# Token blocks of two factors moved by separate transfers, and a projection done in two halves, in a fused two-layer attention kernel

## What is computed

```python
xn  = layernorm(x)
qu  = (xn @ U.T * s).reshape(b, t, C, R)        # U, V: (C*R, 128)
qv  = (xn @ V.T * s).reshape(b, t, C, R)
m   = einsum('bcsr,bctr->bcst', qu, qv)          # scores, 512 x 512 for each channel
h   = sigmoid(m)
o_v = einsum('bcst,bctr->bcsr', h, qv)
o_u = einsum('bcst,bcsr->bctr', h, qu)
x   = x + (o_v @ U + o_u @ V) * s + ffn0(xn)     # ffn0: routed experts, top 64 of 512 tokens each
x   = x + hss_attention(layernorm(x)) + swiglu(layernorm(x))
```

## Time and profile before

| what | value |
|---|---|
| median of three runs | 1467.37 us |
| the profiled execution, device time | 1468.4 us |
| its span, first to last instruction | 1466.6 us |
| mean granted TensorE clock | 0.98 |
| TensorE (PE) busy | 1389.9 us, 95% |
| VectorE (DVE) busy | 903.6 us, 62% |
| ScalarE (ACT) busy | 688.9 us, 47% |
| packets of the DMA queue that SP feeds | 302128, 19.4% of 16 engines' span |

### The profile page before, as it was taken

The page is one execution under the profiler, slowest core; times in us unless marked ns, Lnnn a source line. Parts: engine busy times, 40 slices in busy tenths (PEclk is TensorE's granted clock), DMA queues, the critical chain, the costliest instruction groups (busy, mean ns, idle before and its releaser), DMA issues.

```text
span 1466.6 us, 24503 instructions
## 1 busy us (share of the span) xinstructions
PE 1389.9 (95%) x7806; PEld 793.9 (54%) x7806; DVE 903.6 (62%) x1559; ACT 688.9 (47%) x1058; POOL 44.1 (3%) x41
## 2 busy tenths in 40 slices
PE   6999798899998999999999999999999999999968
PEld 3566444455564555555565555555655555555534
DVE  8868443366655665656655656556555666566657
ACT  3556344444443544454444543454544454454421
POOL 4000400000000000000000000000000000000000
PEclk9999899999999999999999999999999999999988
DMA  6012222112221212221112211221212111221110
GB/s 207 1 31 66 43 35 31 26 29 35 30 30 31 33 27 30 36 32 31 26 26 39 36 29 24 36 34 28 30 29 36 32 26 27 38 30 27 25 30 8
DMA packets 302620, 51.37 MB, mean 35 GB/s; under 512 B 280545, under 2 KB 300769, under 8 KB 302465
## 3 DMA queue, kind: packets, MB, share of 16 engines
q1 hardware_dynamic: 302128, 47.82, 19.4%
q0 software_dynamic: 336, 1.64, 0.3%
HBM read 11.64 MB, written 4.19 MB: 11 GB/s over the span
## 4 chain that ended last, share of the span: by engine, by line
issue 85%; DVE 1%; PE 1%; POOL 1%; ACT 0%; POOLq 0%; DVEq 0%
PE psum L1231 1%; DVE arena L917 0%; DVE arena L923 0%; DVE arena L915 0%; POOL u_w_hl L608 0%; POOL v_w_hl L608 0%; POOL rstd_s L623 0%; POOL up_hl L608 0%; DVE arena L939 0%; PE psum L1575 0%; DVE xn_s L663 0%; POOL u_w_hl L605 0%; POOL v_w_hl L605 0%; DVE x_all L932 0%; POOL up_hl L605 0%
## 5 line engine op out<-in xcount | busy, mean ns | idle before, releaser
L1172 ACT ACTIVATE arena<-psum 128x1024 f32<-128x1024 f32 x504 | 476.0, 1030 | 636.5 <-PE psum L1231 636.3
L1231 PE MATMUL psum<-arena 128*64 128x512 f32 x2016 | 466.0, 605 | 26.0 <-DMA arena<-blocks 14.6
L1231 PEld LDWEIGHTS psum<-arena 128*64 128x64 f32 x2016 | 135.0, 138 | 290.0 <-issue 244.7
L1231 PE MATMUL psum<-u_parts,v_parts 64*128 64x512 f32 x1536 | 199.5, 404 | 11.9 <-issue 11.2
L1231 PE MATMUL psum<-v_parts,u_parts 64*128 64x512 f32 (+1 forms) x1568 | 201.9, 397 | 0.0
L866 DVE TENSOR_SCALAR o_hl<-psum,sums 128x512 fp32r<-128x512 f32 x126 | 94.4, 749 | 162.1 <-PE psum L1231 162.1
L1231 PEld LDWEIGHTS psum<-u_parts,v_parts 64*128 64x128 f32 x1536 | 141.7, 187 | 93.1 <-issue 45.3
L1231 PEld LDWEIGHTS psum<-v_parts,u_parts 64*128 64x128 f32 (+1 forms) x1568 | 145.3, 184 | 81.5 <-issue 51.1
L868 DVE SCALAR_TENSOR_TENSOR o_hl<-psum,sums,o_hl 128x512 fp32r<-128x512 f32 x126 | 94.6, 751 | 4.5
L1121 ACT ACTIVATE arena<-psum 128x512 f32<-128x512 f32 x128 | 77.1, 625 | 18.5 <-PE psum L1231 18.5
L923 DVE TENSOR_TENSOR arena<-psum,arena 128x512 f32<-128x512 f32 x96 | 64.6, 689 | 33.7 <-PE psum L1231 31.7
(11 more groups left out here) (211 smaller groups left out, 1517.0 us busy)
## 6 DMA issues: line engine op xcount, KB each, us to landing
arena<-blocks SPq DMA_DIRECT2D x1008, 32.0 KB, 2.0
x_all<-in_x SPq DMA_DIRECT2D x4, 512.0 KB, 5.4
upper<-in_we SPq DMA_DIRECT2D x8, 256.0 KB, 2.7
expert_rows<-upper SPq DMA_DIRECT2D x16, 128.0 KB, 2.5
xn_s<-expert_rows SPq DMA_DIRECT2D x8, 256.0 KB, 2.9
out<-x_all SPq DMA_DIRECT2D x8, 256.0 KB, 2.5
arena<-in_e POOLq DMA_DIRECT2D x1, 896.0 KB, 5.7
arena<-in_wi POOLq DMA_DIRECT2D x1, 576.0 KB, 5.7
```

Of the source, the lines that this page charges most:

```text
L1172: nc.scalar.activation(th_of(un), psum[:, at:at + 2], ACT.Tanh, scale=0.5 * FACTOR_SCALE ** 2).then_inc(s_th, 2)
L1231: return nc.tensor.matmul(out, lhsT, rhs, start=start, stop=stop)
```

## The change

1. **Tokens.** `raw`, `tok` and `blocks` are split into u and v. Each even half turns v (128x512) and then u (128x512), and SP waits for each and moves it by 16 DMAs of its own, 16 KB each, from 32 to 32 partitions with 4 runs of 32 numbers on each. So a pair has 32 DMAs in place of 16, with the same bytes. `weighted` of the even half waits for v alone, that of the odd half for u. The turn of each waits for the landing of its own move before.
2. **First pair.** The tokens of pair 1 of batch 0 are no more turned and moved: TensorE transposes them (8 transposes into banks 2 and 3, put into the last expert) and ScalarE copies them to `u_tok` and `v_tok`.
3. **Projection.** `pj` becomes `pj0` (v part, o = 0, 3 matmuls) in the odd half of the same pair, and `pj1` (u part, o = 1, 3 matmuls) in the even half of the next, each in its own bank and added to `gT` by an instruction of its own.
4. **Loops on TensorE.** Batch 1 is written out, and batches 2 to 7 are three rounds of a loop with two batches.
5. **Layer 2.** gate and up of chunk 0 move from half 5 to half 3.
6. **Start.** The normalised rows of batches 1, 3, 5 and 7 are made by ScalarE (four ACTIVATE with scale and bias each, and a small VectorE instruction for the bias) and no more by VectorE; the router's products of two batches go to two groups of 32 rows of a bank.

```diff
-FULL_STEPS = {1: [("back", 0)], 2: [("norm", 0)], 3: [("kq", 0), ("v", 0)], 12: [("down", 0)], 15: [("yo", 0), ("yo", 1)]}
+FULL_STEPS = {1: [("back", 0)], 2: [("norm", 0)], 3: [("kq", 0), ("v", 0), ("gate", 0), ("up", 0)], 12: [("down", 0)], 15: [("yo", 0), ("yo", 1)]}
-PREP_IN_HALF = [("pu", "pv", "pj"), ()]
+PREP_IN_HALF = [("pu", "pv", "pj1"), ("pj0",)]
...
-            def move_tokens(i, j, blocks):
-                sp.wait_ge(s_turned, i * PAIRS + j + 1)
-                (16 DMAs, above)
+            def move_blocks(blocks, tok, moved):
+                for r in range(QUARTERS):
+                    for a in range(QUARTERS):
+                        sp.dma_start(tok[32 * r:32 * r + 32, :, 32 * a:32 * a + 32],
+                                     blocks[32 * a:32 * a + 32].rearrange("t (k r c) -> t k r c", k=TB, r=QUARTERS)[:, :, r])\
+                          .then_inc(moved, 16)
+            def move_tokens(i, j):
+                sp.wait_ge(s_vb, i * PAIRS + j)
+                move_blocks(v_blocks, v_tok[:, (j + 1) % 2], s_vt[j])
+                sp.wait_ge(s_ub, i * PAIRS + j)
+                move_blocks(u_blocks, u_tok[:, (j + 1) % 2], s_ut[j])
...
-                nc.vector.transpose(blocks.rearrange("p w t -> p (w t)"), raw.rearrange("p w t -> p (w t)")).then_inc(s_turned, 1)
+                nc.vector.transpose(blocks[:], raw[:]).then_inc(turned, 1)
...
-                        turn(i, j, later_blocks)
+                        turn(i, j, v_raw, v_blocks, s_vb, s_vt)
+                        turn(i, j, u_raw, u_blocks, s_ub, s_ut)
...
-            def project(g, j, bk):
-                pe.wait_ge(s_oe, g * 2)
-                was = (j - 1) % PAIRS
-                passes = [(o, a, b) for o in range(2) for a, b in ((0, 0), (0, 1), (1, 0))]
-                for n, (o, a, b) in enumerate(passes):
-                    ins = mm(bk[:], w_hl[o][:, a, was * D:(was + 1) * D], o_hl[:, o, b], n == 0, n == len(passes) - 1)
+            def project(kind, g, j, bk):
+                o, of = (0, j) if kind == "pj0" else (1, (j - 1) % PAIRS)
+                pe.wait_ge(s_oe, g * 2 + 1 if kind == "pj0" else g * 2)
+                for n, (a, b) in enumerate(((0, 0), (0, 1), (1, 0))):
+                    ins = mm(bk[:], w_hl[o][:, a, of * D:(of + 1) * D], o_hl[:, o, b], n == 0, n == 2)
...
-                if u == 0:
-                    pe.wait_ge(s_moved[(j - 1) % PAIRS], (i + (j > 0)) * MOVED)
+                if blk == 0 and isinstance(i, int) and i == 0 and j == 1:
+                    pe.wait_ge(s_prep_free, prep_index(0, 4) + 1)
+                elif blk == 0:
+                    pe.wait_ge((s_vt, s_ut)[o][(j - 1) % PAIRS], moved_count(i if j else i - 1, (j - 1) % PAIRS))
...
+            prep(0, 3, 1, 0, bank[2])
             attend(*last)
+            prep(0, 4, 1, 0, bank[3])
...
-            with pe.Fori(1, B) as i:
-                iteration(i, True, True)
+            iteration(1, True, True)
+            with pe.Fori(1, B // 2) as m:
+                for n in range(2):
+                    iteration(m * 2 + n, True, True)
```

More of the change, by code:

```diff
@@ L160, in first_middle_of @@
 def first_middle_of(h):
-    work = [w for w in MIDDLE[h] if w[0] in ("pu", "pv", "pj") and w != ("pj", 1)]
+    work = [w for w in MIDDLE[h] if w[0] in ("pu", "pv", "pj0", "pj1") and w != ("pj1", 1)]
     return work + [("sc", 0)] * (h == FIRST_SCATTER_HALF)
@@ L231, in scatter_bank @@
         def scatter_bank(i):
-            return x_bank(("sc", 0), not isinstance(i, int))
+            return x_bank(("sc", 0), not (isinstance(i, int) and i == 0))
         x_all = sb("x_all", [P, B, TB, D])
@@ L527, in _ @@
                 move_rows(E - 4 + par, E // 2 - 2, par)
-            def move_tokens(i, j, blocks):
-                sp.wait_ge(s_turned, i * PAIRS + j + 1)
[L531 to L539, removed]
+            for par in range(2):
+                move_rows(E - 2 + par, E // 2 - 1, par)
             def load_rows(n):
@@ L681, in part_rows @@
                 dve.wait_ge(s_rstd, h + 1)
[L682 to L685, removed]
+                odd, even = h * X_PART + 1, h * X_PART
+                nc.vector.scalar_tensor_tensor(shift1[:, odd], mv1[:, odd, :, 0], -1.0, rstd1[:, odd], ALU.mult, ALU.mult)\
+                  .then_inc(s_shift, 1)
+                if h:
+                    dve.wait_ge(s_xT, even - 1)
+                normalised(xn_g[:, 0], even, mv1[:, even, :, 0:1], rstd1[:, even].unsqueeze(2)).then_inc(s_xn, 1)
             nc.vector.memset(idle[:], 0.0).then_inc(s_ld, N_DVE)
@@ L727, in _ @@
             nc.vector.tensor_tensor(tk_rank, tk_pos, tk_mask, ALU.mult).then_inc(s_tk, 1)
[L729 removed]
+            rank_of, value_of = (rvT[:, a].rearrange("p k (g e b) -> p k g e b", g=2, e=E) for a in range(2))
             def low_rows(n, par):
@@ L855, in add_g @@
                     before = gT[:]
-                if isinstance(i, int) and i == 0 and j == 3:
+                if isinstance(i, int) and i == 0 and (kind, j) == ("pj1", 3):
                     dve.wait_ge(s_scf, 1)
+                if not (isinstance(i, int) and i == 0) and (kind, j) == ("pj0", 0):
+                    dve.wait_ge(s_scf, i + 1)
                 nc.vector.scalar_tensor_tensor(gT[:], bk[:], 0.5 * FACTOR_SCALE ** 2, before, ALU.mult, ALU.add).then_inc(s_pj_free, 1)
@@ L1233, in _, with transposes @@
             pe.wait_ge(s_first, 16 * len(first_consts))
-            def transposes(n, par):
-                pe.wait_ge(s_xn, n + 1)
-                if later(n):
+            def transposes(n):
+                par = n % 2
+                if par == 0:
+                    pe.wait_ge(s_xn, n // 2 + 1)
+                else:
+                    pe.wait_ge(s_xna, n // 2 + 1)
+                if n >= 2:
                     pe.wait_ge(s_xnT, n - 1)
@@ L1241, in transposes, with logits @@
                 ins.then_inc(s_xT, 1)
[L1243 to L1251 removed]
+            def logits(pair):
+                pe.wait_ge(s_xnT, 2 * pair + 2)
+                for g in range(2):
+                    ins = mm(bank[2][g * 64:g * 64 + 32], wr_b[:, pair * 32:pair * 32 + 32], xn1T[:, 2 * pair + g],
+                             pair == 0, pair == B // 2 - 1)
+                return ins
+            transposes(0)
+            transposes(1)
+            pe.wait_ge(s_wr, 2)
+            for n in range(2, B, 2):
+                transposes(n)
+                transposes(n + 1)
+                logits(n // 2 - 1)
+            logits(B // 2 - 1).then_inc(s_lg, 1)
             def early_prep(w, bk):
```

146 lines of the change are left out of this document (85 added, 61 removed).

## The result

The changed kernel takes **1567.5 us** (median of 4 runs, 1565.7 to 1571.6), the kernel before 1466.2 us beside it. The ratio is 1.0695 with a 95% interval of 1.0669 to 1.0721: 101 us, or 7%, slower. The forecast was 1570 us in a range of 1450 to 1612. Of all executions behind this document one, of the run e1_together, lay apart: 2024.7 us, where its seven others took 1469.3 to 1473.2; its ratio leaves that one out.

A forecast was written before the change was run, and what follows sets the result against it. TensorE bounds the kernel before; SP's serial DMA issue would bind after. Along SP: first move 166.3, 62 pairs of 21.6 (1339.2), other DMAs 5.2, landing 1.4, `weighted` 3.65, tail 53.05: 1568.8 us of span, forecast 1570, range 1450 to 1612.

The forecast's parts named there:

- SP becomes the bound, 21.6 us in a pair: SP's token queue: 32 issues of 0.598 us make a pair 21.6 us, where TensorE needs under 19.8; chance 0.72.
- What `expert_rows` and the tokens share is 64 or 32 partitions: SP's issue cost: it goes with partition count, not runs, so it stays near 0.611 us, against 0.387 to 0.432 over 128.
- The 50 ns of the Trainium skill: SP's dispatch: a documentation page's figure, by which 32 issues cost a few us and SP would never bind.
- Start and first pair: Ahead of the loop: 3 us off the start, 7.6 off the first pair, 0.6 off the turn; SP's first move at 166.3.
- Landing and tail: End of the program: tokens land 1.4 us after the last issue; the tail after the last `weighted` is 53.05 us.
- Additions and projection at cost 0: Split projection: the same 6 matmuls and 63 more VectorE additions, 43 us, hide behind SP at cost 0.
- The signs: Expected profile: token groups of 10 to 11 us, SP hardly waiting, TensorE near 88% busy, token waits in nearly all halves.
- Rival 3: VectorE's turn of u waits for the u before to land, adding 1 us a pair: 1632 us; chance 0.04.
- Rival 1: Issues get cheap with the runs, SP does not bind, TensorE's gaps go, 41 us in sum: 1426 us; chance 0.16.
- The 10.8 us of batch 0: Term of the 41 us: batch 0's gaps of 0.98 for DMA and 0.7 for tanh in six pairs go.
- the 11.4 of other token waits: Term of the 41 us: token waits outside batch 0 go, 14.6 less 4.9, and the slow clock behind one.
- The restarts: Term of the 41 us: 4 of 7 restarts of TensorE's loop go, each 1.6 us and some slow clock: 7 us.

The follow-up runs named there:

- e1_together: Changed kernel with u and v turned by one instruction and moved together again, 16 DMAs of 32 KB a pair: 1472.3 us, ratio 1.0055.
- e2_before_split: Kernel before with only the token split: v and u turned one after the other, each moved by 16 DMAs of 16 KB: 1614.8 us, ratio 1.1033.
- e4_u_on_gpsimd: Changed kernel with u's 16 DMAs a pair issued by GpSimd, v's left on SP: 1458.8 us, ratio 0.9956.
- The shapes: Kernel of its own, without the computation: SP issues groups of 16 SBUF to SBUF DMAs, one shape a group; 140.9 us, without meaning as a kernel time.
- e12_split_whole: Changed kernel with the projection whole again in the even half, v and u still apart, 32 issues a pair: 1572.2 us, ratio 1.0731.
- e6_projection_whole: e1_together with the projection whole in the even half: 1465.6 us, ratio 0.9997.
- e9_u_gpsimd_whole: e4_u_on_gpsimd with the projection whole in the even half: 1452.0 us, ratio 0.9911.
- e13_both_queues: e9_u_gpsimd_whole with each of v and u issued half by SP and half by GpSimd, 8 issues each: 1445.9 us, ratio 0.9860.
- e14_before_two_queues: Kernel before with only 8 of the 16 token DMAs of a pair issued by GpSimd, from the second pair on: 1454.1 us, ratio 0.9924.
- e5_one_batch_loop: e1_together with TensorE's loop of one batch a turn, three more restarts: 1484.8 us, ratio 1.0140.

## Why the prediction was right, and where its steps were wrong

*SP becomes the bound, 21.6 us in a pair: right.* From the first v group to the last the period measured 21.64 a pair, loads and stores within it; the prediction's 62 x 21.6 + 5.2 = 1344.4 us stands against 1341.5. The issue of 0.598 us measured 0.601. That the sums agree so closely is in part luck. The prediction took the rare long issues to come as often for each issue, and a group of the kernel before at 10.98 us (redone from its trace: 10.95). But of the issues over 0.8 us 57 fell on v and only 5 on u; a v group lasts 10.94 us and a u group 10.34, so the groups sum to 16 us less than forecast, while the pauses between groups and the loads and stores take some 10 us more (22 in all). Both directions were tested, by e1_together (95 us less) and e2_before_split (151 us more), and e4_u_on_gpsimd shows that it is the queue.

*"What `expert_rows` and the tokens share is 64 or 32 partitions": wrong reason for a right number.* The shapes show 0.60 to 0.70 for 128 partitions as well. The median issue is at 0.59 to 0.70 for every kind of DMA between places in SBUF on SP in these runs, so the cheap rows of 0.39 to 0.43, loads from memory, were no bound for these at all. Why loads are cheaper, and why the store of `expert_rows` (0.616) is not, no run tests.

*The 50 ns of the Trainium skill* (DMA: Bandwidth & Descriptors, Anatomy of one DMA) for a dispatch, which the prediction set against its sum: the runs decide for the row, at 0.60 us for an issue on SP and 0.55 on GpSimd, whose path the page describes. The rule of the Trainium skill to coalesce many small transfers (same page, Rules for kernel authors) holds here, by e1_together against the changed kernel.

*Start and first pair: right within 2 us, by two misses that offset each other.* The first `weighted` has no wait, and SP's first group begins at 167.80 for 166.3. TensorE is done with `pv` at 158.95, 4.4 us sooner than before, not 3. But VectorE is late: the two instructions that split u take 1.62 and 2.74 us there (0.43 and 0.69 a pair later), and its turn of v starts at 167.07, 4.5 us behind the end of `weighted`, where it was 1.5 us in the kernel before (176.21). A new wait of TensorE of 2.39 us on `o_hl` at 167.21 was not foreseen either and has the same cause.

*Landing and tail.* Landing 1.4 is right: the u group ahead of 1509.33 is issued by then, and the last `weighted` begins at 1510.66. The tail from its end is 1565.6 - 1514.31 = 51.3 us for 53.05.

*Additions and projection at cost 0: right under this bound* (e12_split_whole), and 7 us without it (e6_projection_whole, e9_u_gpsimd_whole). The text held that without SP's cover the additions would only eat into "some 7 us free per pair" of VectorE. What the split cost then came from TensorE: its matmuls (5.3 us) and its waits on `o_hl` (6.6 us in e1_together, 4.1 in e6_projection_whole).

*The signs.* Right: groups of mostly 10 to 11 us with almost no gap, SP hardly waiting. Wrong: TensorE waits for tokens in 69 of some 126 halves, not in nearly all, since in the longer halves its own work is longer than SP's 10.6 us; and it is 90% busy, not 88%, as slow-clock work counts as busy.

*Rival 3* had its mechanism in the trace, not its price. VectorE's turn of u waits for the u before to land:

```profile
DVE u_blocks L810 <- DMA arena<-u_blocks: 221.8, 61, 5.3
```

SP still never waits for it, so it is off the path.

*Rival 1's 1426 us: wrong, and this is the largest error,* though it did not enter the forecast. With SP free the sum of gaps was 41 us (one term is misreckoned: 0.98 and 0.7 in six pairs are 10.1, not 10.8); e1_together took 9 us more than the 1463.3 us of the kernel before beside it. Three terms failed. The 10.8 us of batch 0 and the 11.4 of other token waits were counted as gaps of TensorE, but they are the slack of a chain through SP's 16 issues, which the change leaves as long. The projection's split costs 7 in place of giving. The restarts were undervalued (7 for four against 12.5 measured for three), but TensorE, relieved of them, waits for the same chain. Had the issues become cheap with the runs, this chain would have been shorter, which e13_both_queues imitates, with the projection whole; it takes 1446 us.

## What to carry to other kernels

An engine that issues DMAs does so one after the other, and the busy shares don't show it: multiply the issues in a period by the measured issue time, and compare that with the period, before any transfer is cut in two. The same issues are also a latency: where a chain through the issues sets the length of a period, as in batch 0 here, only a shorter chain helps, and closing other gaps of TensorE in the period just moves the wait. Where a second engine has an idle queue, give it half of the issues; here that alone gave 0.8%, and with the useful parts of the change 1.4%.

## What the hardware showed that was not expected

- The issue of a DMA from SBUF to SBUF on SP takes, in the median, 0.59 to 0.63 us over 32 partitions for 1 to 16 runs and 0.60 to 0.70 over 128 for 1 to 8, with 0.04 between two; so 64 KB over 128 partitions in whole rows (0.601) cost the queue what 16 KB over 32 do.
- GpSimd's queue issues the same DMA in 0.548 us (0.582 with the 8 runs of u and v together, in e14_before_two_queues), a little less than SP. SP's issues are no slower beside it: groups of 8 on SP take 5.1 us, half of 10.4. GpSimd issuing alone no run shows. From issue to landing it is 2.4 to 2.6 us in that kernel, where it was 2.0.
- Three restarts less of TensorE's long loop were worth 12.5 us, about 4 each, where the trace of e5_one_batch_loop lists waits of 0.79 to 1.18 us at its restarts; the rest is, as far as seen, in the longer waits for tokens and the slower `weighted` behind them.
